# A two-layer transformer block: the row maxima of the first attention transposed once per group of four heads

## The reference, cut to what matters

```
q, k = apply_rope(split(x @ Wq.T + bq)), apply_rope(split(x @ Wk.T + bk))
att = einsum('bhqd,bhkd->bhqk', q, k) / sqrt(16)
att = softmax(where(tril, att, -inf), axis=-1)
y = einsum('bhqk,bhkd->bhqd', att, v) @ Wo.T + bo
```

## Time and profile before

| | us |
|---|---|
| median of 3 runs (lowest to highest) | 1579.58 (1578.19 to 1579.97) |
| the profiled execution | 1577.66 |
| its span, first to last instruction | 1575.7 |
| PE busy | 1484.3 (94%) |
| DVE busy | 1097.1 (70%) |
| ACT busy | 824.2 (52%) |

### The profile page before, as it was taken

The page is one execution under the profiler, slowest core; times in us unless marked ns, Lnnn a source line. Parts: engine busy times, 40 slices in busy tenths (PEclk is TensorE's granted clock), DMA queues, the critical chain, the costliest instruction groups (busy, mean ns, idle before and its releaser), DMA issues.

```text
span 1575.7 us, 29502 instructions
## 1 busy us (share of the span) xinstructions
PE 1484.3 (94%) x10998; PEld 1069.2 (68%) x10998; DVE 1097.1 (70%) x1876; ACT 824.2 (52%) x1196; POOL 806.3 (51%) x1003
## 2 busy tenths in 40 slices
PE   3879999999999999999999999999999999999995
PEld 2546666666676767577767777777777777777774
DVE  5677787877777786855565748757586675774765
ACT  2344445354535444535556666656666565665641
POOL 4133535344444444334656657656576565755742
PEclk8788999999999999999999999999999999999998
DMA  7334343434343333110200010100101001000000
GB/s 164 61 42 68 42 82 42 82 41 80 40 80 40 67 41 66 70 68 1 74 14 1 1 41 1 41 1 1 40 0 40 0 0 40 0 15 13 1 27 13
DMA packets 46498, 60.82 MB, mean 39 GB/s; under 512 B 4912, under 2 KB 31952, under 8 KB 46416
## 3 DMA queue, kind: packets, MB, share of 16 engines
q1 hardware_dynamic: 45552, 59.03, 19.1%
q10 hardware_dynamic: 864, 0.66, 0.1%
HBM read 25.83 MB, written 8.39 MB: 22 GB/s over the span
## 4 chain that ended last, share of the span: by engine, by line
PE 86%; DVE 8%; ACT 3%; issue 2%; POOL 1%; DMA 0%; SPq 0%; POOLq 0%; DVEq 0%; ACTq 0%
PE psum L353 41%; PE psum L1745 9%; PE psum L1710 9%; PE psum L1761 6%; PE psum L999 5%; PE psum L1733 4%; PE psum L985 4%; PE psum L954 3%; DVE l_rowmax L823 2%; ACT l_probs L750 1%; PE psum L360 1%; PE psum L961 1%; PE psum L969 1%; PE psum L1019 1%; PE psum L1008 1%
## 5 line engine op out<-in xcount | busy, mean ns | idle before, releaser
L750 ACT ACTIVATE l_probs<-psum 128x512 f32<-128x512 f32 (+1 forms) x384 | 181.0, 524 | 207.7 <-PE psum L985 206.8
L1529 DVE RECIPROCAL l_att<-psum 128x512 f32<-128x512 f32 x64 | 214.6, 3354 | 55.1 <-PE psum L1733 50.8
L823 DVE TENSOR_REDUCE l_rowmax<-psum 128x2 f32<-128x1024 f32 (+3 forms) x256 | 200.5, 817 | 54.4 <-PE psum L961 54.0
L1445 ACT ACTIVATE l_probs<-psum 128x1024 f32<-128x1024 f32 (+1 forms) x192 | 163.7, 880 | 121.6 <-PE psum L1710 117.6
L227 POOL TENSOR_TENSOR l_pool_holder<-expo 128x1 f32<-128x1 f32 x128 | 26.0, 203 | 371.2 <-ACT l_probs L1451 199.0
L1520 DVE TENSOR_TENSOR l_qk_lo<-psum,l_qk_hi 128x1024 fp32r<-128x1024 f32 x64 | 77.9, 1217 | 176.2 <-ACT l_qk_hi L1435 176.2
L232 POOL TENSOR_SCALAR_AFFINE_SELECT l_probs<-l_probs 128x256 f32<-128x256 f32 (+1 forms) x384 | 176.4, 491 | 0.0
L1451 ACT ACTIVATE l_probs<-l_probs 128x2048 f32<-128x2048 f32 (+1 forms) x128 | 157.7, 1267 | 0.0
L1745 PE MATMUL psum<-l_probs,l_v 128*64 128x512 f32 (+3 forms) x1024 | 149.9, 435 | 0.0
L1745 PEld LDWEIGHTS psum<-l_probs,l_v 128*64 128x64 f32 x1024 | 71.4, 137 | 87.2 <-issue 75.3
L1377 POOL TENSOR_TENSOR l_keysum<-l_probs 128x768 f32<-128x768 f32 x62 | 113.9, 1836 | 6.2
(11 more groups left out here) (210 smaller groups left out, 4089.2 us busy)
## 6 DMA issues: line engine op xcount, KB each, us to landing
l_kT<-l_roped_hi SPq DMA_DIRECT2D x64, 128.0 KB, 4.2
l_qT<-l_roped_hi SPq DMA_DIRECT2D x64, 128.0 KB, 6.1
l_xin<-in_x SPq DMA_DIRECT2D x8, 512.0 KB, 4.1
l_kT<-l_roped_lo SPq DMA_DIRECT2D x32, 128.0 KB, 5.4
l_qT<-l_roped_lo SPq DMA_DIRECT2D x32, 128.0 KB, 6.6
l_x<-in_x SPq DMA_DIRECT2D x8, 512.0 KB, 4.0
x_mid<-l_x SPq DMA_DIRECT2D x8, 512.0 KB, 3.0
l_xin<-x_mid SPq DMA_DIRECT2D x8, 512.0 KB, 4.7
```

The lines of the kernel that those rows point to most:

```text
L750: ring_s.free(nc.scalar.activation(probs[:, SLOT[p], e, c0:c1], ring_s.unit(*use)[:, 0:c1 - c0], ACT.Exp, scale=HD0 ** -0.5), *use)
L823: reduced = nc.vector.tensor_reduce(rowmax[:, t, a // 2, :, a % 2], ring_d.unit("max", a, k)[:, :, c0:c0 + (t + 1) * P], mybir.AxisListTyp ...
L1445: ring_s.free(nc.scalar.activation(probs[:, p % 2, :, c0:c1], ring_s.unit("score", p, u)[:, :, 0:c1 - c0], ACT.Tanh, scale=HD1 ** -0.5 / C ...
L1529: ring_d.free(nc.vector.reciprocal(att[p % 2][:], ring_d.unit("den", p)), "den", p)
```

## The change

The maxima are kept as pair, then tile, so that one transpose of 128x16 does a group; it lies in a bank as 16 rows of 128. The copy takes 16x128 in place of 4x512, and each placing DMA reads 8 partitions of 128 values in place of 2 partitions of 512, into the same row of `qT`.

```diff
-    maxT = sb("maxT", [4, T], F32R)
+    maxT = sb("maxT", [4 * NT, P], F32R)
-    rowmax = sb("rowmax", [P, NT, PAIRS // 2, 2, 2])
+    rowmax = sb("rowmax", [P, PAIRS // 2, 2, 2, NT])
...
-                sp.dma_start(qT[row:row + 1, 2 * g:2 * g + 2, :].bitcast(F32),
-                             maxT[2 * e:2 * e + 2, :].bitcast(F32)).then_inc(max_placed.sem, 16)
+                sp.dma_start(qT[row:row + 1, 2 * g:2 * g + 2, :].bitcast(F32).rearrange("r a (t q) -> r (a t) q", q=P),
+                             maxT[2 * NT * e:2 * NT * (e + 1), :].bitcast(F32)).then_inc(max_placed.sem, 16)
...
-            ring_s.free(nc.scalar.activation(maxT[:], ring_s.unit("maxT", g)[0:4, :], ACT.Copy, scale=-1.0), "maxT", g)
+            ring_s.free(nc.scalar.activation(maxT[:], ring_s.unit("maxT", g)[0:4 * NT, 0:P], ACT.Copy, scale=-1.0), "maxT", g)
...
-                reduced = nc.vector.tensor_reduce(rowmax[:, t, a // 2, :, a % 2], ...
+                reduced = nc.vector.tensor_reduce(rowmax[:, a // 2, :, a % 2, t], ...
...
-            for t in range(NT):
-                last = nc.tensor.transpose(ring_s.unit("maxT", g)[0:4, t * P:(t + 1) * P],
-                                           rowmax[:, t, g, :, :].rearrange("p e a -> p (e a)"), ident[:])
+            last = nc.tensor.transpose(ring_s.unit("maxT", g)[0:4 * NT, 0:P], rowmax[:, g, :, :, :].rearrange("p e a t -> p (e a t)"), ident[:])
```

More of the change, by code:

```diff
@@ L485, in phase1 @@
[L485 to L498, removed]
+        "load_x": {(): -22.18},
+        "x_stats": {(): -16.77},
+        "x_rstd": {(): -16.19},
+        "x_norm": {(): -13.77},
@@ new lines, in phase1 @@
+        "x_T": {(0,): -13.4, (1,): -13.38},
+        "x_T_hi": {(0,): -10.63, (1,): -10.31},
+        "x_T_lo": {(0,): -13.69, (1,): -11.44},
+        "rope": {(0,): -8.25, (1,): -6.57, (2,): -0.36, (3,): 4.89},
+        "roped": {(0,): -8.64, (1,): -6.58, (2,): 0.38, (3,): 5.06},
+        "turned": {(0,): -7.88, (1,): -2.3, (2,): 3.55, (3,): 6.96},
+        "rope_sum": {(0,): -11.08, (1,): -7.11, (2,): -0.99, (3,): 4.49},
+        "rope_hi": {(0,): -4.35, (1,): 1.13, (2,): 7.26, (3,): 9.17},
+        "rope_lo": {(0,): -10.12, (1,): -4.56, (2,): 3.15, (3,): 4.55},
@@ new lines, in phase1 @@
+        "att_T_lo": {(0,): 33.42, (1,): 33.51},
+        "o": {(0,): 34.58, (1,): 34.6},
+        "o_out": {(0,): 34.27, (1,): 35.89},
+        "x1_T": {(0,): 41.01, (1,): 41.03},
+        "x1_T_hi": {(0,): 42.34, (1,): 42.44},
+        "x1_T_lo": {(0,): 41.03, (1,): 41.33},
+        "o_stats": {(): 36.37},
+        "o_rstd": {(): 35.67},
+        "residual": {(): 45.84},
+        "o_norm": {(): 36.6},
+        "x1_stats": {(): 38.3},
+        "x1_rstd": {(): 36.29},
+        "x1_norm": {(): 38.69},
@@ L821, in row_max @@
             for t, c0 in MAX_UNITS[k]:
-                reduced = nc.vector.tensor_reduce(rowmax[:, t, a // 2, :, a % 2], ring_d.unit("max", a, k)[:, :, c0:c0 + (t + 1) * P],
+                reduced = nc.vector.tensor_reduce(rowmax[:, a // 2, :, a % 2, t], ring_d.unit("max", a, k)[:, :, c0:c0 + (t + 1) * P],
                                                   mybir.AxisListType.X, ALU.max)
@@ L1192, in phase2 @@
-        "out": {(): 46.57},
-        "gate_b": {(): 53.6},
-        "gate": {(): 46.55},
-        "x4_stats_b": {(): 53.86},
-        "x4_stats": {(): 47},
-        "x4_rstd_b": {(): 68.84},
-        "x4_rstd": {(): 48.67},
-        "x4_norm_b": {(): 57.88},
-        "x4_norm": {(): 48.05},
-        "store_b": {(): 52.21},
-        "store": {(): 51.32},
+        "load_x": {(): -20.61},
+        "x_stats": {(): -18.34},
+        "x_rstd": {(): -14.19},
+        "x_norm": {(): -4.22},
+        "x_T": {(0,): -1.52, (1,): -1.31},
@@ new lines, in phase2 @@
+        "x3_stats": {(): 36.7},
+        "x3_rstd_b": {(): 40.52},
+        "x3_rstd": {(): 38.21},
+        "x3_norm_b": {(): 40.49},
+        "x3_norm": {(): 39.19},
+        "x3_T_b": {(): 39.03},
+        "x3_T": {(): 38.73},
+        "x3_T_out_b": {(): 39.58},
+        "x3_T_out": {(): 39.4},
+        "mix": {(0,): 40.79, (1,): 42.18},
+        "mix_hi": {(0,): 39.93, (1,): 42.27},
+        "mix_lo": {(0,): 40.59, (1,): 42.97},
+        "r": {(): 42.31},
+        "r_out": {(): 43.76},
+        "key": {(): 42.24},
@@ L1203, in phase2 @@
+        "key_out": {(): 42.92},
+        "square": {(): 43.82},
+        "kact_hi": {(): 42.94},
+        "kact_lo": {(): 44.72},
+        "out": {(): 45.81},
+        "gate_b": {(): 47.11},
+        "gate": {(): 46.22},
+        "x4_stats_b": {(): 48.84},
+        "x4_stats": {(): 47.03},
+        "x4_rstd_b": {(): 69.15},
+        "x4_rstd": {(): 47.83},
+        "x4_norm_b": {(): 57.77},
+        "x4_norm": {(): 47.56},
+        "store_b": {(): 59.95},
+        "store": {(): 44.24},
     }
```

244 lines of the change are left out of this document (104 added, 140 removed).

## The result

The changed kernel takes 1568.86 us (median of 4 runs, 1568.51 to 1569.28), the kernel before in the same comparison 1578.88 (4 runs, 1577.99 to 1579.97). The ratio is 0.9935, 95% interval 0.9923 to 0.9947: 10.0 us less. The forecast was 1562 with a range of 1554 to 1575, so direction and range hold and 7 us of the forecast gain are missing. The profiled execution took 1568.51 us, its span is 1566.8. Executions of one kernel can lie some 6 us apart by the start alone: in a second profile of the changed kernel (e5, 1574.94 us) PE's clock was at 1.2 GHz for 38 us from 24 us on, in this one for 20, and `max.0.0` of batch 1 came at 105.05 us instead of 98.89.

The account below looks back on a forecast made before the run. PE was taken as the bound, except for a 12 us DVE stretch per phase 1 turn. Transposes -10.5, phase 2 -3.6, phase 1 order -0.5, `rope.3` -1.8 and end -1.3 gave -17.7 us: 1562 us, range 1554 to 1575.

Parts of the forecast that it names:

- The transposes, -10.5: PE's queue, 32 groups: three removed transposes each give back their start spacing of 0.109 us, 10.5 us in all.
- rival D: PE's transposes are worth their duration, 26.1 instead of 10.5 us, giving 1546 us; chance 0.02.
- PE busy down by some 26 us: Sign expected in the profile page: PE's busy time falls by some 26 us and its span by 17.
- The copy, 0: ACT's copy of the maxima: 0.31 us shorter per group, left out of the sum because ACT is 47% busy.
- The placing DMAs, 0: DMAs placing the maxima: landing still 1.68 us, hidden with 1.6 us to spare before `score.4.0`, so cost 0.
- Rival B: At `score.4.0` in each batch the placed maxima come late; slower than before if landing exceeds 5.5 us; chance 0.06.
- `rope.3`, -1.8, and the closing up: Phase 1: `rope.3`'s 0.53 us wait goes in 6 or 7 turns (3.4 us); half counted as pieces close up elsewhere.
- Rival C: PE's granted clock falls in all phase 1 turns instead of half, plus 1 us at the start: 1566 us; chance 0.10.
- Phase 2, -3.6: PE in phase 2: five fewer changes of matmul kind at 0.095 us, 0.47 us per turn over 7.5 turns.
- a wait appears in phase 2's turns, where nothing can absorb it: Sign of a wrong forecast: a new PE wait in phase 2, where a turn has 0.15 us of idle PE.
- The start, 0: First turn: half the warm pieces and two DVE weight pieces move; taken as 0, bounds -3 and +3 us.
- The end, -1.3: Very end: a DVE norm and `gate_b` move into waits for POOL, 2 x 0.65 us gained.

Follow-up runs that it names:

- e5: The changed kernel timed again without further edits: median 1569.6 us, ratio 0.9943 to the kernel before; its profiled execution took 1574.94 us.
- e2: The changed kernel with the old layout of the maxima (four transposes, 4x512 copy) and the new order kept: 1577.5 us, 0.9993 of the kernel before.
- e6: The changed kernel with four transposes side by side per group and a 16x512 copy in place of 16x128: 1577.2 us, 0.9986 of the kernel before.
- e3: The changed kernel with the one transpose per group issued four times into the same place: 1573.9 us, 0.9975 of the kernel before.
- e7: The changed kernel with ten idle-time matmuls per phase 1 turn in PE's gaps of the DVE stretch: 1564.7 us, 0.9921 of the kernel before.
- e1: The kernel before with the new layout of the maxima alone, all places in the old order: 1577.7 us, 0.9992 of the kernel before.
- e8: The changed kernel with phase 2, the seam between the phases and the end in their old places: 1572.7 us, 0.9960 of the kernel before.
- e9: The kernel before with idle-time matmuls in PE's two long gaps of a phase 1 turn's DVE stretch: 1578.1 us, 0.9991 of the kernel before.
- e10: The kernel before with the new layout in the old order and fillers in PE's two long phase 1 gaps: 1572.0 us, ratio 0.9956.
- e4: The changed kernel with two of its three heat pieces of a phase 1 turn moved later: 1575.7 us, 0.9987 of the kernel before.

## Why the prediction was right, and where it was not

- *The transposes, -10.5.* The spacing, not the duration, is the price: three removed transposes gave 0.18 to 0.32 us back, never 3 x 0.27, and rival D fell. "Since each `maxT` lies on the chain I count all of it" failed: in the new order `maxT.1` stands in the DVE stretch, where nearly all of its share is PE's free time (the prediction says so two paragraphs on and didn't take it off), and `maxT.2` gave 0.19. 0.73 per turn in turns with a fall (by the table above 1.49 - 0.63 = 0.86 in turns without), not 1.31. The Trainium skill (TensorE: Matmul & The Clock Gate, Part 4: PE-mode transpose) puts some 275 ns on one; the duration here is 277, but the runs show that it is no price of a transpose among others. "PE busy down by some 26 us" took the durations once more: a run of four counts 0.60 us of busy time and one alone 0.28, so that the rows gave 10.5 us for the transposes; with all other changes it was 16.4.
- *The copy, 0.* This is the term that was mis-sized. Its length came out as worked (259 ns, 274 said). But "ACT is 47% busy, so its time is not in the sum" looked at the engine's load and not at who waits for the bank. In the new order two scores per turn would wait for the long copy; the short one saves 0.63 us per turn (e2 and e6, each beside e3). By luck the two errors nearly cancel: 0.73 + 0.63 = 1.4, against the 1.31 counted.
- *The placing DMAs, 0.* Right: PE waits for none. Rival B fell.
- *`rope.3`, -1.8, and the closing up.* The wait went in all five turns (2.7 us). Of it and the changes of kind 0.06 per turn remain with the old layout, 0.50 with the new: `maxT` now waits for ACT's exponentials (4.1 us, was 1.7), and so do the scores.
- *PE's clock.* Rival C, given 0.10, is what happened in the middle turns: "if it falls in all turns instead of half". Four of five turns fell, at 80.05 against 81.4, or 1.4 us each; before two fell, at some 0.9 each. 5 x 1.55 = 7.75 us of gain, less 4 x 1.4 - 2 x 0.9 = 3.8, leaves 4.0; measured 4.1. e7 shows it by taking the falls away. The forecast itself had no term for the falls; but in the changed kernel they come at the end of the stretch in which PE waits for DVE, and this stretch is part of the change: up to `max.5.0` PE was idle for 2.6 of 8.4 us in it before (382.40 to 390.81) and for 3.0 of 8.6 after.
- *Phase 2, -3.6.* Measured -0.19 per turn instead of -0.47. The step that failed is "a change costs about 0.095 us", as one price for every place. It holds at `o.4` and `key`, which no longer follow a piece of another kind and are each 0.10 shorter. But the timeline of `score.1.0` and `score.1.1`, before and changed, shows the same instructions with other spacings, behind `pv.7` before and behind `score.0.2` after:

```profile
1028.66 0.40 PE L1710 MATMUL psum<-l_qk_lo,l_qk_hi 64*128 64x512 f32 x2
1028.89 0.39 PE L1710 MATMUL psum<-l_qk_hi,l_qk_lo 64*128 64x512 f32 x2
1029.12 0.22 PE L1710 MATMUL psum<-l_qk_hi 64*128 64x128 f32 x2
1029.18 0.28 PE L1710 MATMUL psum<-l_qk_lo,l_qk_hi 64*128 64x128 f32 x2
```
```profile
1019.79 0.40 PE L1708 MATMUL psum<-l_qk_lo,l_qk_hi 64*128 64x512 f32 x2
1020.03 0.40 PE L1708 MATMUL psum<-l_qk_hi,l_qk_lo 64*128 64x512 f32 x2
1020.41 0.33 PE L1708 MATMUL psum<-l_qk_hi 64*128 64x128 f32 x2
1020.58 0.28 PE L1708 MATMUL psum<-l_qk_lo,l_qk_hi 64*128 64x128 f32 x2
```

  From the last 512-column pair to the 128-column pair 0.38 us instead of 0.23, and then 0.17 instead of 0.06, without a wait that the trace names. Why is open. `x_T.1` is followed by a score 0.17 us later than it was by `o.2`.
- *A wait in the last batch, not in the sum.* The prediction named it as a sign of being wrong ("a wait appears in phase 2's turns, where nothing can absorb it"), and one appeared. What PE waited for in the changed kernel from `qk.0` of batch 7 to the end of its attention (1407.94 to 1525.4 us; 0.3 us for ACT left out). Before, PE waits for nothing there:

```profile
PE psum L1721 <- DVE l_att L1527: 1.5, 1, 1.5
```

  The last batch has no scores of a next one between `pv.6` and `den.7`. Before, `o.4` stood there with 1.6 us; the new order has it ahead of `den.6`, and `den.7` waits 1.47 us for the unit that DVE's reciprocal frees. All nine traces with the new phase 2 have this wait, the five with the old one (before, e1, e8, e9, e10) have none.
- *The start, 0.* It gave 3.7 us in the profiled pair, and 0.7 with the layout alone (e1), 1.2 with the order alone (e2), and -2.4 in the changed kernel's second profile: it varies by 6 us between two executions of one kernel, so that no worth of the new start can be told.
- *The end, -1.3.* Nearly right, but hidden by that wait. Counted from `qk.0` of batch 7, DVE's statistics of the attention's result (`o_stats`) start 1.46 us later than before (117.43 against 115.97); behind the moved `x3_norm` (0.73 us, now in the wait, at 1533.62) the delay is 1.03 us, behind the moved gate 0.34. The two moves gave 1.1 us, and the stretch is still 0.4 us longer.

The two sets of causes are shown to different degrees. That the clock took back 3.8 us in the middle turns and that the copy is on the path are shown by taking each away (e7, e6). The wait of the last batch is shown by the runs with and without the new phase 2. Where the turns of phase 2 lost 0.3 us each is only located.

## What to carry to other kernels

Price a short producer on an idle engine by who waits for the buffer that it frees, not by the engine's load; a new order can put it on the path, and only then does shortening it pay, so that layout and order can each be worth nothing alone and 10 us together. Where PE waits for another engine, look at the granted clock just behind the wait before a shortened turn is counted as gained, and fill such gaps with idle matmuls that end before the gap does and hold up no piece that the other engine waits for. Compare turns that have the same granted clock. Read the waits of the first and last turn by themselves: a piece that covers a wait there can be one that a steady turn doesn't need.

## What the runs showed of the hardware

**A filler in a gap was free, one that held up a piece for DVE was not.** Ten more matmuls of 512 columns per turn cost no measurable time in e7 (80.05 us, as the changed kernel's turns without a fall) and gave 1.2 us by the clock. e4 has as many matmuls as the changed kernel, but two of them between `score.1.0` and `max.4.0`, which came 0.46 us later; its turns, all with a fall, were 0.4 us longer (81.87 against 81.4).

**DVE's instructions took longer beside POOL's.** In phase 2 the same DVE instructions from SBUF took longer in the changed kernel, those with a PSUM source did not. DVE's groups by form, 810 to 1400 us, before and changed:

```profile
L345 DVE TENSOR_SCALAR l_xin<-l_xin,l_x_mv,l_x_rstd 128x256 f32<-128x256 f32 x24 | 14.5, 663 | 0.0
L345 DVE TENSOR_SCALAR l_xn<-psum,l_o_mv,l_o_rstd 128x256 f32<-128x256 f32 x24 | 10.8, 514 | 0.0
```
```profile
L345 DVE TENSOR_SCALAR l_xin<-l_xin,l_x_mv,l_x_rstd 128x256 f32<-128x256 f32 x24 | 25.9, 1136 | 0.0
L345 DVE TENSOR_SCALAR l_xn<-psum,l_o_mv,l_o_rstd 128x256 f32<-128x256 f32 x24 | 10.8, 513 | 0.0
```

The new places put some of them beside POOL's sums over SBUF. Timelines of DVE and of POOL in the changed kernel, around one such place:

```profile
1308.16 2.28 DVE L1648 TENSOR_TENSOR l_x<-l_x,l_xn 128x1024 f32<-128x1024 f32 x1
```
```profile
1281.82 0.73 POOL L1379 TENSOR_TENSOR l_keysum<-l_keysum,l_probs 128x256 f32<-128x256 f32 x1
...
1308.06 1.30 POOL L1377 TENSOR_TENSOR l_keysum<-l_keysum,l_probs 128x512 f32<-128x512 f32 x1
1309.44 1.60 POOL L1379 TENSOR_TENSOR l_keysum<-l_keysum,l_probs 128x256 f32<-128x256 f32 x1
```

DVE's addition takes 2.28 us where a lone one of this size takes 1.23 (L1554 at 1252.40). It looks as if it stood until POOL's 1.30 us ended at 1309.36 and ran until 1310.44, and POOL's next instruction, 0.73 us elsewhere, stood until then and took 1.60. The Trainium skill (SBUF — State Buffer, SBUF: two separate sides) says that the two share a pair of SBUF ports, which whichever of them starts first holds for its whole instruction (on DVE's side one with two SBUF inputs, as here, is among those that need it); these times agree with that, though no run here took one of the two away. It cost no time, since PE is busy for 100.86 of 101.02 us there.
